# The last attention's scores from three bf16 terms along one head's contraction

## The reference, cut to what matters

```python
q = einsum('oc,bct->bot', Wq, x) + bq[None, :, None]      # c = 128, t = 256
k = einsum('oc,bct->bot', Wk, kv) + bk[None, :, None]
v = einsum('oc,bct->bot', Wv, kv) + bv[None, :, None]
# 16 heads of 8 rows each
attn = einsum('bhqd,bhdk->bhqk', q * 8 ** -0.5, k)
attn = softmax(where(kv_mask, attn, -inf))
mean = attn @ v;  std = sqrt(relu(attn @ (v * v) - mean * mean))
out = (instance_norm(x, mask) * std + mean) * mask
```

## Time and profile before

| | |
|---|---|
| median of three runs | 1072.5 us (1072.28 to 1078.0) |
| profiled execution | span from first to last instruction 1069.8 us; its whole time is not listed beside it |
| PE busy | 965.6 us, 90% |
| DVE, ACT, POOL busy | 51%, 44%, 26% |
| granted clock of PE, mean | 0.975 |
| transfers | 60.14 MB, mean 56 GB/s |

### The profile page before, as it was taken

One profiled execution on the slowest core, in us unless ns is written; L12 is line 12 of the kernel. 1 busy time (PEld: TensorE's weight loads), 2 busy tenths in 40 slices (PEclk: granted clock), 3 DMA queues, 4 the chain that ended last, 5 costly groups with the idle time before them and its releaser, 6 DMA issues.

```text
span 1069.8 us, 21418 instructions
## 1 busy us (share of the span) xinstructions
PE 965.6 (90%) x8560; PEld 600.5 (56%) x8560; DVE 545.0 (51%) x1036; ACT 471.2 (44%) x808; POOL 275.1 (26%) x389
## 2 busy tenths in 40 slices
PE   7989999999999999999999999999999999985673
PEld 5566663666456664666636664556646666344430
DVE  3343565455645565445644556455654556543433
ACT  2424453453534545345534545345543455333223
POOL 0230230342211621233302422116212333023201
PEclk9999999999999999999999999999999999988867
DMA  9300230001300202102300113002121022002001
GB/s 369 147 2 1 80 104 23 18 22 64 109 30 6 80 28 87 36 2 84 109 19 19 40 46 109 31 5 80 40 76 36 2 85 99 18 19 79 6 1 40
DMA packets 29057, 60.14 MB, mean 56 GB/s; under 512 B 9376, under 2 KB 21024, under 8 KB 24096
## 3 DMA queue, kind: packets, MB, share of 16 engines
q1 hardware_dynamic: 28960, 58.77, 15.1%
HBM read 53.52 MB, written 5.24 MB: 55 GB/s over the span
## 4 chain that ended last, share of the span: by engine, by line
PE 74%; DVE 11%; issue 7%; ACT 4%; POOL 2%; DMA 1%; SPq 0%; DVEq 0%; ACTq 0%; POOLq 0%
PE GP L598 6%; PE GP L999 6%; PE PV L737 6%; PE GP L1010 6%; PE GP L600 5%; PE SC L805 5%; DVE nm L1455 4%; PE SC L720 4%; PE GP L983 3%; PE PV L776 3%; PE PV L930 3%; PE GP L822 2%; PE GP L605 2%; PE SC L917 2%; PE MX L653 2%
## 5 line engine op out<-in xcount | busy, mean ns | idle before, releaser
L1455 DVE TENSOR_REDUCE nm<-MX 128x2 bf16<-128x512 f32 (+1 forms) x352 | 227.1, 690 | 147.2 <-PE MX L659 59.0
L1229 ACT ACTIVATE Pr<-SC,bcol 128x1024 f32<-128x1024 f32 x64 | 71.2, 1113 | 137.0 <-PE SC L805 126.1
L1786 POOL TENSOR_TENSOR Psum<-Pr 128x512 f32<-128x512 f32 x64 | 81.4, 1272 | 173.6 <-ACT Pr L1229 173.6
L598 PE MATMUL GP<-zP,W 128*128 128x128 f32 x512 | 106.9, 291 | 7.1 <-DMA W<-w 7.1
L1229 ACT ACTIVATE Pr<-SC 128x1024 f32<-128x1024 f32 x64 | 65.3, 1020 | 81.9 <-PE SC L720 42.4
L600 PE MATMUL GP<-uP,W 128*128 128x128 f32 x512 | 100.3, 278 | 0.0
L598 PEld LDWEIGHTS GP<-zP,W 128*128 128x128 f32 x512 | 78.8, 194 | 28.5 <-issue 26.7
L1270 ACT ACTIVATE Pr<-SC,bcol 128x512 f32<-128x512 f32 x96 | 60.7, 684 | 58.6 <-PE SC L917 58.6
L1754 POOL TENSOR_TENSOR stat<-stat,half 128x1 f32<-128x1 f32 x24 | 13.7, 569 | 267.7 <-DVE stat L1635 172.5
L600 PEld LDWEIGHTS GP<-uP,W 128*128 128x128 f32 x512 | 79.2, 195 | 0.0
L1010 PE MATMUL GP<-WB,work 128*128 128x256 f32 x256 | 62.5, 394 | 10.5 <-DVE work L1583 10.5
(11 more groups left out here) (202 smaller groups left out, 1733.8 us busy)
## 6 DMA issues: line engine op xcount, KB each, us to landing
WA<-w1a SPq DMA_DIRECT2D x8, 1024.0 KB, 4.8
WB<-w1b SPq DMA_DIRECT2D x8, 1024.0 KB, 7.2
WA<-w2a SPq DMA_DIRECT2D x8, 1024.0 KB, 5.0
WB<-w2b SPq DMA_DIRECT2D x8, 1024.0 KB, 7.1
W<-w SPq DMA_DIRECT2D x6, 1024.0 KB, 10.0
scratch<-U SPq DMA_DIRECT2D x16, 256.0 KB, 2.0
C<-scratch SPq DMA_DIRECT2D x96, 32.0 KB
zP<-z_in SPq DMA_DIRECT2D x8, 128.0 KB, 4.4
```

Source lines behind the costliest of these rows:

```text
L598: pe.matmul(dst, W0[:, piece, 2 * s, at:at + P], zP[:, s * P:s * P + P], start=True, stop=False)
L1229: act.activation(Pr[:, n % 4:n % 4 + 2, :], SCP[:], ACT.Exp, bias=bcol[:, 3 + k % 2:4 + k % 2] if L else 0.0, scale=8.0 ** -0.5 if L else ...
L1455: dve.tensor_reduce(dst, MX[(n + i) % 2][:].rearrange("p (a k) -> p a k", a=a), AX_X, ALU.max, negate=True).then_inc(mx_done, 1)
L1786: pool.tensor_tensor(Psum[:, c % 4, :].rearrange("p (a l) -> p a l", l=D), two[:, :, 0:D], two[:, :, D:2 * D], ALU.add)\
```

## The change: what it does

Queries and keys of L3 are each split into three bf16 terms (high, middle, low) that add up to the float32 value. They lie in a tile `parts` of [128, 3, 256]. SP stores it into a DRAM tile, waits, and loads it three times into the new tiles Kx and Qx: rows 0 to 71 hold, for every head, 9 combinations of terms by 8 dimensions, so that a matmul over these rows sums the nine products. Row 72 of Kx is the mask of keys against ones in Qx, rows 96 to 99 are the four heads' one-hot rows in Kx against the shifts in Qx. The masked tiles, the bias of the Exp and the matmuls for mask and shift go away.

The turn ("T") of L3 now copies four rows of shifts to all four heads of the group at once. The list `BOTH` is ordered anew: the first maxima of L3 stand after the scores of step (0, 7), and the "B" units stand elsewhere. The key terms are made by ACT (high), DVE (rest) and POOL (middle, low), the query terms all by DVE. Kx and Qx take room in SBUF: W0 keeps five pieces, the fifth of which is loaded anew for every pair of `vp` projections; `work` has two parts instead of three, with G in the place of T.

```diff
-        (0, 5, [(3, 0, 0)], []), (0, 6, [(3, 0, 2)], []), (0, 7, [("den", 2), (3, 0, "T")], [(3, 1, 0)]),
-        (3, 0, [], [(3, 1, 2)]),
-        (3, 1, [("den", 3), (3, 1, "T"), ("recip", 1, 0)], [(0, 0, "B")]),
-        (3, 2, [(0, 1, "B"), ("recip", 1, 1)], [("out", 0), (3, 2, 0)]),
-        (3, 3, [("out", 1), (3, 2, 2)], [("out", 2), ("out", 3), (3, 2, "T")]),
-        (3, 4, [(0, 2, "B")], [(3, 3, 0)]),
-        (3, 5, [(3, 3, 2), ("out", 4)], [("out", 5), (3, 3, "T")]),
-        (3, 6, [(0, 3, "B")], []), (3, 7, [("out", 6), ("out", 7)], [])]
+        (0, 5, [], [(0, 0, "B")]), (0, 6, [], [(0, 1, "B")]),
+        (0, 7, [(3, 0, 0)], [(3, 0, 2), ("den", 2)]),
+        (None, 0, [], [(3, 0, "T"), (3, 1, 0)]),
+        (3, 0, [], [(3, 1, 2)]),
+        (3, 1, [("den", 3), ("recip", 1, 0), ("recip", 1, 1)], [(3, 1, "T"), (3, 2, 0)]),
+        (3, 2, [("out", 0), ("out", 1)], [(3, 2, 2), ("out", 2)]),
+        (3, 3, [(3, 2, "T"), ("out", 3)], [(0, 2, "B"), (3, 3, 0)]),
+        (3, 4, [], [(3, 3, 2), (0, 3, "B")]),
+        (3, 5, [("out", 4)], [("out", 5), (3, 3, "T")]),
+        (3, 6, [("out", 6)], [("out", 7)]), (3, 7, [], [])]
...
-        W0 = sb("W0", [P, 6, 4, 512])
+        W0 = sb("W0", [P, 5, 4, 512])
...
+            def load_values(n):
+                sp.wait_ge(s_V0, 2 * n)
+                sp.dma_start(W0[:, 4], w0[4 + n % 2]).then_inc(ld_w0v, 16)
+
+            def terms(b, dst, scr, ready, stored, landed, key_side):
+                sp.wait_ge(ready, b + 1)
+                sp.dma_start(scr.rearrange("i d (h l) -> (d h) i l", l=D), parts[:]).then_inc(stored, 16)
+                if key_side:
+                    sp.wait_ge(s_msk, N_MSK * b + 3)
+                    sp.dma_start(dst[72:73], b3row[0:1, :].unsqueeze(1).to_broadcast([1, NH, D])).then_inc(landed, 16)
+                sp.wait_ge(stored, 16 * b + 16)
+                for j in range(3):
+                    src = scr[j:j + 1].to_broadcast([3, 8, NH * D]) if key_side else scr
+                    sp.dma_start(dst[24 * j:24 * j + 24], src).then_inc(landed, 16)
 
             def body(b):
                 sp.wait_ge(s_x1, b + 1)
                 load_mlp(w2a, w2b)
+                if not is_last(b):
+                    load_values(2 * b + 3)
                 if not is_first(b):
                     store_batch(b - 1)
+                terms(b, Kx, k_parts, s_K3l, st_k, ld_kx, True)
+                terms(b, Qx, q_parts, s_Q3l, st_q, ld_qx, False)
                 if not is_last(b):
-                    sp.wait_ge(s_x3, b + 1)
                     load_mlp(w1a, w1b)
                     load_inputs(b + 1)
                     if b + 2 < B:
                         load_z(b + 2)
+                        load_values(2 * b + 4)
...
 # maxima_pair3
+                    for i in range(2):
+                        wait(pe, *mx_bank_taken(n + i))
+                        h = HG * g + u + i
+                        for s in range(2):
+                            mm = pe.matmul(MX[(n + i) % 2][:, s * D:s * D + D], Qx[0:96, h, s * P:s * P + P],
+                                           Kx[0:96, h, :], start=True, stop=True, skip_group_check=True)
+                        mm.then_inc(mx_full[(n + i) % 2], 1)
...
 # scores3
                 for j in range(2):
+                    pe.wait_ge(p_ready, SC_AT[b, 3, 2 * k] - 1 + j)
+                    for e in range(2):
+                        h = HG * g + 2 * j + e
+                        mm = pe.matmul(SC[j][:, e * D:e * D + D], Kx[0:100, h, kc * P:kc * P + P], Qx[0:100, h, :],
+                                       start=True, stop=True, skip_group_check=True)
+                    mm.then_inc(sc_full, 1)
...
 # DVE
+            def rest(g, bias, dst, high):
+                dve.wait_ge(*high)
+                return dve.scalar_tensor_tensor(out=dst, in0=g[:, 0:D], scalar=col(bias), in1=parts[:, 0, :],
+                                                op0=ALU.add, op1=ALU.subtract)
+
+            def queries3(b, o):
+                g = take(o, "q3")
+                dve.wait_ge(st_k, 16 * b + 16)
+                dve.tensor_scalar(parts[:, 0, :], g[:, 0:D], col("bq"), None, ALU.add).then_inc(s_Q3h, 1)
+                rest(g, "bq", rest_q, (s_Q3h, b + 1)).then_inc(s_Q3r, 1)
+                dve.wait_ge(s_Q3r, b + 1)
+                dve.tensor_copy(parts[:, 1, :], rest_q).then_inc(s_Q3m, 1)
+                dve.wait_ge(s_Q3m, b + 1)
+                dve.tensor_tensor(parts[:, 2, :], rest_q, parts[:, 1, :], ALU.subtract).then_inc(s_Q3l, 1)
...
+                    elif L == 3:
+                        dst = Qx[96:100, HG * g:HG * g + HG, :]
+                        src = turned[96:100, 0:D].unsqueeze(1).to_broadcast([HG, HG, D])
...
 # POOL, before power(b, 3)
+            def keys3(b):
+                pool.wait_ge(s_K3r, b + 1)
+                pool.tensor_copy(parts[:, 1, :], rest_k).then_inc(s_K3m, 1)
+                pool.wait_ge(s_K3m, b + 1)
+                pool.tensor_tensor(parts[:, 2, :], rest_k, parts[:, 1, :], ALU.subtract).then_inc(s_K3l, 1)
...
 # PE, projections vp0 to vp3
-                    pe.wait_ge(ld_w0[4 + w], 16)
+                    pe.wait_ge(ld_w0v, 16 * (2 * k + w + 1))
```

More of the change, by code:

```diff
@@ L110, in mix @@
             units(b, end)
-            sc.extend((b + (L == 0), L, 2 * k + i) for i in range(2))
+            if L is not None:
+                sc.extend((b + (L == 0), L, 2 * k + i) for i in range(2))
     def banks0(b, names):
@@ L226, in build @@
         Q12 = work[:, 0:8 * P].rearrange("p (h l) -> p h l", l=P)
-        Q3 = work[:, 8 * D:12 * D].rearrange("p (t l) -> p t l", l=D)
-        X, T, G = (work[:, 1024 * i:1024 * i + 1024] for i in range(3))
+        X, T = (work[:, 1024 * i:1024 * i + 1024] for i in range(2))
+        G = T
         zP = sb("zP", [P, D])
@@ L261, in build @@
         V2 = sb("V2", [P, 17 * 32])
-        K3 = sb("K3", [P, 2, D])
-        K3b = sb("K3b", [P, 2, D], BF16)
+        parts = sb("parts", [P, 3, D], BF16)
+        Qx = sb("Qx", [P, NH, D], BF16)
+        Kx = sb("Kx", [P, NH, D], BF16)
         V3 = sb("V3", [P, 2, NH, 32])
@@ L540, in load_inputs @@
                 sp.dma_start(m3row[:], mask3[b].to_broadcast([P, D])).then_inc(ld_msk, 16)
-                for c in range(2):
-                    sp.dma_start(m3col[:, c:c + 1], mask3[b][:, c * P:c * P + P].rearrange("o p -> p o"))\
-                        .then_inc(ld_msk, 16)
             def load_z(b):
@@ L1134, in body @@
                 pe.matmul(g[:, 0:D], W3[:, 0, :], x3[:], start=True, stop=True).then_inc(full, 1)
-                mixed(b, range(4, 16) if more else range(8), make03)
+                mixed(b, range(4, len(BOTH)) if more else range(8), make03)
                 mix_end(b)
@@ L1205, in sums @@
                                GP[order_of(b).at(f"u{i}")[0]][:], ACT.Copy).then_inc(s_U3, 1)
-            def queries3(b, which):
-                g = take(order_of(b), "q3")
-                act.wait_ge(s_Q3b, b + 1)
-                for dst, t in which:
-                    ins = act.activation(dst[:, t, :], g[:, 0:D], ACT.Identity, scale=hmask[:, 4 + t:5 + t],
-                                         bias=col("bqm", t))
-                    if t % 2:
-                        ins.then_inc(s_Q3, 1)
             def mixed(b, steps):
@@ L1373, in keys3 @@
                     g = take(o, "k3")
-                    for e in range(2):
-                        ins = act.activation(K3[:, e, :], g[:, 0:D], ACT.Identity, scale=hmask[:, 8 + e:9 + e],
-                                             bias=col("bkm", e))
-                    ins.then_inc(s_K3, 1)
+                    wait(act, st_q, 16 * b)
+                    act.activation(parts[:, 0, :], g[:, 0:D], ACT.Identity, bias=col("bk")).then_inc(s_K3h, 1)
                 attention12(b, 2, 0.25, keys3)
@@ L1393, in body @@
                     cast(b + 1, 3)
-                mixed(b, range(4, 16) if more else range(8))
+                mixed(b, range(4, len(BOTH)) if more else range(8))
                 mix_end(b)
@@ L1658, in body @@
                     maxima(b + 1, 0, 1, "T")
+                rest(take(o, "k3"), "bk", rest_k, (s_K3h, b + 1)).then_inc(s_K3r, 1)
                 quotient(b, 2, 0)
@@ L1682, in body @@
                     maxima(b + 1, 0, 3, 0)
-                g = take(o, "q3")
-                for t in range(2):
-                    ins = dve.tensor_scalar(Q3b[:, t, :], g[:, 0:D], col("bq"), hmask[:, 4 + t:5 + t],
-                                            ALU.add, ALU.mult)
-                ins.then_inc(s_Q3b, 1)
-                mixed(b, range(4, 16) if more else range(8))
+                queries3(b, o)
+                mixed(b, range(4, len(BOTH)) if more else range(8))
                 mix_end(b)
```

158 lines of the change are left out of this document (60 added, 98 removed), and 4 rows, old and new, of the table TAKEN.

## The result

The changed kernel takes 1145.95 us (median, 1143.4 to 1150.96) against 1072.51 us beside it on the same chip: ratio 1.068, 95% interval 1.064 to 1.071, so 73 us slower. The forecast was 1102 (1068 to 1136): the direction was right, the size fell outside the range. The profiled execution has a span of 1149.2 us against 1069.8 before. It is the slowest of the four (1150.96), so some 5 us of the 79.4 between the two profiles are the draw of one execution.

A forecast was written before the change was run, and what follows sets the result against it. The prediction took PE's instruction stream, with almost no slack, to bound the kernel. It summed 1069.8 + 27 + 7 + 3 - 5 - 3 + 2.7 = 1101.5, said as 1102 us, range 1068 to 1136.

The forecast's parts named there:

- Part 1: scores3: four bf16 matmuls in series take 0.43 to 0.44 a step instead of 1.08, saving PE 41 us (31 to 41).
- Part 2: maxima3: four bf16 matmuls in series take 0.43, against 0.22 for mask and 0.22 for products; nothing gained or lost.
- Part 3: After x1, PE waits 3.8 us for W0's reload queued behind w2a and w2b; 27 us over seven batches (22 to 32).
- Part 4: After the reload's wait PE's clock falls, costing 1.0 us a batch, 7 us in all (0 to 12).
- Part 5: Terms around x3: DVE's query chain 1.67, key term +3 us in all; loads on twelve engines (fast) or three (slow).
- Part 6: Mixed section: the order of waits leaves 0.7 of 5.1 us a batch, 5 us faster (9 slower to 50 faster).
- Part 7: Last batch: terms make the first maxima pair 6.5 us later, cheaper scores still end it earlier: -3 us.
- B: Mixed section: terms land late on three engines, PE waits 409.9 to 413.2; 28 us more, 1130; chance 0.27.
- C: Mixed section: the scores' saving goes through, 5.1 a batch, with the reload's wait kept; 1068.5; chance 0.08.
- D: After x1: the reload lands in time as well as the scores' saving going through; 1034, faster; chance 0.10.
- E: The reload lands in time, but the scores' saving is given back; 1067.5; chance 0.05.
- A: Whole kernel: the main forecast, its parts as summed to 1102; own range 1088 to 1118; chance 0.50.

The follow-up runs named there:

- e3: The kernel before with only the two reloads added, at the same places of SP's queue, into the slots the values already have; 1115.86 us, ratio 1.041.
- e4: The kernel before with the fp32 pass of scores3 taken in bf16 (exactness left out), orders, copies and turns as before; 1052.19 us, ratio 0.982.
- e2: The changed kernel with load_values(2b+3) issued ahead of SP's wait for x1 (the early reload); 1107.65 us, ratio 1.032.
- e8: e4 with the changed kernel's order of the mixed section; no terms, no reload, old turn's copy; 1088.2 us, ratio 1.015.
- e10: e2 with the L3 steps from 1 on reordered (interleaved tail): turn (3,1) ahead of reciprocals, reciprocals, out chunks and spreads spaced out; 1070.36 us, ratio 0.997.
- e13: e12 with the turn's copy cut to 4x256 from 4x1024 (shift of three of each four heads left out); 1061.05 us, ratio 0.988.
- e12: e10 with one output chunk moved behind the turn in step 3 and one in step 5; 1069.13 us, ratio 0.996.
- e5: e2 with the turn's copy cut to 4x256 from 4x1024 (shift of three of each four heads left out); 1089.84 us, ratio 1.017.
- e11: e10 with the maxima pairs of group 3 ahead of both spreads, which move to steps 5 and 6; 1076.22 us, ratio 1.004.
- e9: e2 with the turn (3,1) placed ahead of the two reciprocals instead of behind them and pv3(0); 1092.94 us, ratio 1.020.
- e6: e2 with the stores and loads of the terms only in the first batch; 1093.75 us, ratio 1.022.

## Why the forecast had the direction and not the size

By its own sum the forecast was +29 against the profiled 1069.8; the profile has +79.4. The 50 us between them, some 5 of which are the draw of the profiled execution:

| part | forecast | profile | more |
|---|---|---|---|
| 3, wait for the reload, seven batches | 27 | 28.6 | 2 |
| 4, the clock after it | 7 | 14.6 | 8 |
| 5, key term on DVE (0.4 a batch) | 3 | 3.2 | 0 |
| the reload ahead of the first x1 | 0 | 3 | 3 |
| 6, mixed section, to the next x1 | -5 | 24 | 29 |
| 7, last batch | -3 | 5.4 | 8 |

The 3 us ahead of the first x1 are a term that the prediction put at nothing: PE waits 1.82 us there for the second half of the value weights, since both halves now share one slot, and the clock falls behind that wait; e3, where they have a slot each, has no such wait and reaches x1 after 113.1 us instead of 116.1.

Each cause alone, by medians: the cheap scores -20 (e4 and before), the reload +38 to +44 (e2, e3), the order +36 (e8 and e4; 37 by e2 and e10), the wide turn +8 (e13 and e12) and, by a profile, the landing in the last batch +8. With the key term's 3 that is +73 to +79 for a measured +73.

**Part 1, scores3: the step right, its worth half.** A step takes 0.44 between starts, as forecast, and PE has 41 us less to do. Alone and in the old order that is worth 20.

**Part 2, maxima3: right.** 0.45 a pair, forecast 0.43.

**Part 3, the reload's wait: right.** 28.6 us for 27, within 22 to 32.

**Part 4, the clock after it: right mechanism, half its size.** From x1 to x3 seven batches take 299.6 us; with the early reload they take 256.4. Of the 43.2 between, 28.6 are the waits; the 14.6 that are left I take for the time at half clock after them, 2.1 a batch (in the old kernel, e3, 29.8 and 14.1). I had taken 1.0 from a stretch with clock 0.90 and bounded it at 12 in all; here the clock is 0.66 to 0.83.

**Part 5, terms: right for steady batches, with no margin.** DVE's chain took 1.78 from 429.82 (I had 1.67), store to load 2.07 (2.2). PE could start 11.0 us after the start of x3, where the fast case said 9.2 and the slow one 14.9. The landing was late by 1.8 and in six of the seven batches still in time, by 0.8 or so; in the seventh PE waited 0.33. Such a wait comes and goes: e5's profile has three, of 0.31, 0.41 and 2.27 us. In the last batch nothing hides the landing, as these rows show (x3, the loads, the first pair):

```profile
1094.10 0.42 DVE L1681 SCALAR_TENSOR_TENSOR x<-GP,res 128x256 f32<-128x256 f32 x1 [4.78 <-PE GP L1019]
...
1099.26 1.14 SPq L573 DMA_DIRECT2D Qx<-q_parts  x3
...
1105.14 1.01 PE L678 MATMUL MX<-Kx,Qx 96*128 96x256 bf16 x4 [9.80 <-issue]
```

**Part 6, the mixed section: the step that failed, and what it lacked is again the clock.** I had laid the rows end to end and found -0.7 a batch. In us from the end of x3, beside a batch of the early reload (x3 ends at 406.27), whose mixed section is the changed one:

| | forecast | early reload |
|---|---|---|
| turn (3,0) copied | 15.9 | 16.4 |
| turn (3,1) copied | 21.5 | 22.5 |
| turn (3,2) copied | 26.4 | 29.5 |
| turn (3,3) copied | 34.8 | 38.9 |
| `kp0` | 39.1 | 42.1 |

Up to (3,1) the walk holds: it has the reciprocals ahead of that turn, and the copy's 0.69 (measured 0.70). It parts from the trace behind the wait for (3,1). PE has stood for 1.8 us, and the next 3 us of its work go at half clock. The walk priced every piece from rows at full clock and had no term for what a wait does to it. A second, smaller error: the spread (0,3) waits 1.50 for two reductions (L782 in the rows above), and in three of the seven batches of the changed kernel the clock fell behind that wait again.

How much is which? The stretch from x3 to x1 was 88.1 before and should have been 87.4. After, the best batches take 90.0 to 90.4, at 0.98. By e5, e8, e11 and e12, where one execution has batches at 1.00 and at 0.98, the step between the two is 0.9 to 2.0, mostly 1.5 (in e9 it is 1.2 to 1.6 in four batches, but one at 0.98 takes the same 88.5 as the one at 1.00); so at full clock the changed stretch takes an estimated 88.7. The walk's own error is then 1.3 a batch, 9 of the 29 us, and the clock has 20. With Part 4's 8 the clock is some 28 of the 50 us that I missed. That estimate rests on batches of other kernels; what e10 shows without one is that an order in which PE's waits are short has six batches of seven at 1.00, and takes 86.4. Short waits are no guarantee: e12, with the same order up to the turn (3,1), has three batches at 0.98.

Nor did the old order have the saving in it in full: its stretch with cheap scores is 85.5 (e4), 2.6 of 5.1 us, since PE then waits for DVE's reductions. I had priced the new order against the old one with the dear scores, and never asked what the old order would do with the cheap ones.

**Part 7, the last batch: sign wrong, and its saving three times too large.** +5.4 instead of -3. The first pair stands 8.7 us later than before (11.04 against 2.33 after x3), of which I had 6.5. The other 6 us are a saving that I had too large. From the first pair to the end I had 9.4 us less than before; the trace has 3.3 less, and e6, where the first pair stands 3.3 after x3, has 3.6. PE does come back at half clock after idling for 9.8 us: scores3 takes 1.03 to 1.06 until 1120, where it takes 0.60 at full clock. But so it did before the change: from the first pair to the end the clock is half for 30 us now, for 27 then and for 28 in e6, so it explains under 2 us. What holds the last batch's steps otherwise was not tried.

**Rivals.** B, late terms, fell in steady batches but for one wait of 0.33, by a margin of 0.8 us. C, D and E fell: the reload was not in time, and the saving did not go through. A's mechanisms all showed, and the clock was larger than its range had room for.

**Better than both.** With the reload ahead of x1 and the interleaved tail the change is back at the kernel before: e12 at 0.996, faster than before by less than a measurement is sure to tell. Its mixed section gains 2.2 a batch at full clock; the key term gives 3 back, the last batch 5.4 and the stretch ahead of the first x1 1.7, and three batches at 0.98 give 3.6 more. The short turn's 1061 leaves out part of the work, and e4's 1052, the fastest of all, the exactness.

## What to carry to other kernels

A PE saving is worth what the engines that feed it let through: try it alone and in place (here by casting one product) before buying it with space, loads and a new order. Put a reload on the queue where the old contents die, not beside loads that happen to be near; that place was worth 38 us. Where engines hand over in turn, give each wait of PE of more than a microsecond a second price for the half clock behind it, which behind the reload's waits was about half as much again, and look for DVE work that stands ahead of a turn that PE needs.

## What the runs showed of the hardware

**A wait is paid twice, and not each time alike.** One program in one execution has stretches of equal work that take 89.3, 90.9 and 92.4 us at clocks of 1.00, 0.98 and 0.96 (e8). At each reload's wait of 3.8 to 5.0 us the clock fell in all seven batches. In the mixed section of the changed kernel it fell around the wait for the turn (3,1), 1.0 to 1.8 us, in all seven, and behind the spread's 1.50 in three; in e8 it fell behind a wait of 1.54 for that turn in four of seven. In e10, whose mixed section has no wait above 0.8, it fell in none of six; in e12, whose order is the same up to the turn (3,1), it fell there in three of six, behind waits of 0.57 and 0.42. So a short wait makes the loss rarer and does not rule it out. The Trainium skill (TensorE: Matmul & The Clock Gate, section HAM oscillation — how this bites in real kernels) says that waits for transfers between bursts of matmuls bring the engine back to its lower clock again and again; the trace agrees, with 4.97 us of waiting and then 1.85 instead of 1.12 for a pair of matmuls; here 1.82 us of waiting for DVE did it too, with 1.00 instead of 0.60 for a step of scores3.

**Loads of the same size into 24 rows ran on twelve transfer engines for the queries and on three for the keys.** Stretches of the changed kernel's last batch (columns as in the first stretches): two microseconds in which the query terms alone move, the four microseconds around them, and eight with the key terms:

```profile
1101.00:1102.00 1.00, 0.00 (x0) 0.00 (x0) 0.00 (x0) 0.00 (x0) 0.00 (x0) 0.50 0.93 197
1102.00:1103.00 1.00, 0.00 (x0) 0.00 (x0) 0.00 (x0) 0.00 (x0) 0.00 (x0) 0.50 0.81 164
1100.00:1104.00 4.00, 0.00 (x0) 0.00 (x0) 0.00 (x0) 0.00 (x0) 0.00 (x0) 0.50 0.66 147
1075.00:1083.00 8.00, 4.37 (x19) 3.38 (x18) 3.25 (x9) 0.81 (x2) 1.26 (x2) 0.79 0.17 72
```

A packet counts whole in the stretch in which it starts, so the short stretches overshoot; over four microseconds the share is 0.66, 10.6 engines of sixteen with the start and the end of the loads in it. Three engines would show 0.19; that is why rival B did not come. The packets of the trace say twelve: twelve are in flight most of the time, and each of the three loads ends with twelve packets of 4 bytes, where the store before them has sixteen. The rate is 147 GB/s against the weights' 436, and so the terms landed 1.8 us later than the fast case. Besides the four engines that are missing, a packet of 8 KB takes 0.64 us in the median and one of the weights 0.31; why was not tried.

The keys' loads are rival B's slow case as it was priced: three packets in flight, three packets of 4 bytes at the end of each, 0.31 us a packet, 590 KB in 8.2 us (I had 82 GB/s and 7.2 us). They come early enough to cost nothing. In the source (`terms`) the keys' side is one term broadcast to three, the queries' side the three terms as they lie. The rule of the Trainium skill that I had weighed (DMA: Bandwidth & Descriptors, section Why a DMA increments its semaphore by 16 and not by 1) gives three or, merged, twelve engines for such a load, and the trace agrees with both: the dense source runs as the merged one, the broadcast as the one that is not.
